# First stage of a gated cross-attention block worked by halves of its batches, with its loads reordered

## Chip, cores and metric

One core of a Trainium2 chip runs the whole program; the other cores are idle. The metric is device time in microseconds (us), the median over runs. The trace is of one profiled execution.

## What is computed

Two layers of cross-attention and a feed-forward part each. Only the first attention matters here (8 batches, 100 tokens, 361 context rows, width 256):

```
h = layernorm(x)                                   # x (8, 100, 256)
s = (h Wq^T + bq)(ctx Wk^T + bk)^T / 16            # ctx (8, 361, 256)
p = softmax(where(mask, s, -1e9))
x = x + tanh(g_xattn[0]) * (p (ctx Wv^T + bv))
x = x + tanh(g_ffn[0]) * ffn(layernorm(x))         # experts, next stage
...                                                # second layer
```

## The kernel before

Each engine has its own instruction list, written out by hand, and waits on semaphores where it needs another's result. The first stage avoids the keys: it forms `fold` = Wq^T Wk / 16 once (L1499, called from the `mm` helper: four products of 256 columns), and the small vectors `foldv` and `fold0` from the biases (ten products with one column each). With them the score of a batch is `tT` times the raw context, where `tT` = fold^T `hT` + `foldv`, plus a constant per token, `ccol`.

In order, the stage does this:

- **SyncE** issues all loads in one queue: `x` (100 partitions of 8 KB), `consts`, the three weights `wq0`, `wk0`, `wv0` (tile `arena` in the trace), `bqk`, the gates, the row `bv`, `mask8`, and then the context of batches 0-1, 2-3 and 4-7 (`GROUPS`, `load_context`): each as two pieces of its transpose (`ctxT`, in `ctxbuf`) and three of its rows (`ctxN`, in `big`, 121, 121 and 119 partitions). After that come rows and weights of the next stage.
- **VectorE** takes the statistics of all eight batches (L1068, L1056), GpSimd raises the variance to -1/2 (L606), and VectorE writes the normed rows `hN` (L1063).
- **TensorE** waits for all of `ld_w0` (64) and `ld_const` (64), forms the fold and the bias products, transposes `hN` in four groups of two batches (`ln_pe`, L1509), each of which ScalarE copies to `hT` (L763), and then makes four query groups of 400 columns (`tT`, copied by ScalarE, L776), two rows of constants (`cT`, one output row of 400 columns each, L780) and eight tiny transposes that turn the constants into `ccol` (L1547, L1081).
- Then a loop over i runs scores(i) against `ctxT`, softmax on VectorE and ScalarE (L1090 to L1094, L795), and for earlier batches the transpose of the probabilities, the mix with the context rows, its transpose and the product with `wv0`. Before scores(0), (2) and (4) TensorE waits for the context group (`ld_ctx0` to `ld_ctx2`).

A product of float32 shows as two MATMUL records in the trace, a transpose as one. `arena`, `ctxbuf` and `big` are shared by many tiles.

## Time and profile before

| | us |
|---|---|
| median of 3 runs | 556.81 (556.79 to 558.48) |
| the profiled execution's own time | 556.68 |
| its span in the trace | 554.9 |
| TensorE busy | 503.3 (91%) |
| VectorE busy | 277.3 (50%) |
| ScalarE busy | 188.4 (34%) |
| GpSimd busy | 160.9 (29%) |
| hardware DMA queue, share of 16 engines | 42.2% |

The span is what the trace covers; the 1.8 us beside it lie outside the records. The busy share says which engine sets most of the time; what the change is worth is read from the first 33 us.

### The profile page before, as it was taken

Reading aid. Unit: us, or ns where it says so; the run is one execution under the profiler, and the core shown is the slowest. Engines: PE = TensorE matmul, PEld = TensorE weight load, DVE = VectorE, ACT = ScalarE, POOL = GpSimd, SP = SyncE. Lnnn points to the kernel's source line nnn. Section 1 sums busy time; section 2 is a strip of 40 time slices with the busy share of each in tenths; the row PEclk is TensorE's granted clock in tenths of the full one; section 3 lists DMA queues with packets and bytes.
Section 4 is the critical chain, followed back from the end, with each engine's and each line's share of the span. In section 5 each row is a group of like instructions: output and inputs, shape, how many; then the busy total and the mean of one; then the engine's idle time right before and its main releaser. Section 6 shows DMA issues by size and latency. Waiting matters only on the chain.

```text
span 554.9 us, 9313 instructions
## 1 busy us (share of the span) xinstructions
PE 503.3 (91%) x3392; PEld 334.6 (60%) x3392; DVE 277.3 (50%) x664; ACT 188.4 (34%) x443; POOL 160.9 (29%) x179
## 2 busy tenths in 40 slices
PE   1989889899999889999999989899999988999992
PEld 1636565445556558887877767778867564444441
DVE  2436553112222767565576877988743214323452
ACT  1233331121112436555555554646652103110000
POOL 3122005001016306422241562543200666000232
PEclk9799978999999999999999999999999997999997
DMA  8978992269976987887555209300000233002100
GB/s 220 220 200 282 389 335 57 80 215 395 386 258 210 257 187 211 217 203 186 144 138 138 55 2 332 124 2 2 2 1 0 68 129 121 18 17 68 27 11 24
DMA packets 51790, 82.33 MB, mean 148 GB/s; under 512 B 10340, under 2 KB 40428, under 8 KB 51643
## 3 DMA queue, kind: packets, MB, share of 16 engines
q1 hardware_dynamic: 45967, 69.58, 42.2%
q0 software_dynamic: 5776, 12.13, 6.9%
q8 instruction: 29, 0.48, 0.4%
q14 instruction: 18, 0.15, 0.1%
HBM read 66.87 MB, written 15.15 MB: 148 GB/s over the span
## 4 chain that ended last, share of the span: by engine, by line
PE 73%; DVE 12%; issue 4%; DMA 4%; ACT 2%; SPq 1%; POOL 1%; POOLq 0%; DVEq 0%; ACTq 0%
PE pb L1499 68%; DVE hN L1063 2%; DVE nmx L1360 1%; DMA row_bv<-in_L_xattn_bv 1%; DMA qx_dram<-big_r 1%; DVE prob L1363 1%; PE pb L1910 1%; DMA hN<-yt_dram 1%; DVE bn L1050 1%; POOL rstd L606 1%; PE pb L1770 1%; DVE ctxbuf L1290 1%; PE pb L1680 1%; DVE nmx L1268 1%; DVE x L1211 1%
## 5 line engine op out<-in xcount | busy, mean ns | idle before, releaser
L1499 PE MATMUL pb<-split 128*100 128x362 f32 (+2 forms) x320 | 77.5, 326 | 4.0 <-DVE nmx L1268 2.7
L1499 PE MATMUL pb<-ring,big 128*116 (+1 forms) x232 | 76.8, 578 | 1.1 <-ACT big L822 1.1
L1268 DVE TENSOR_REDUCE nmx<-pb 100x1 f32<-100x361 f32 x128 | 62.8, 527 | 21.4 <-PE pb L1499 20.9
L1499 PEld LDWEIGHTS pb<-split 128*100 128x100 f32 (+2 forms) x320 | 55.5, 181 | 13.7 <-DVE nmx L1268 5.3
L1499 PEld LDWEIGHTS pb<-ring,big 128*116 128x116 f32 (+1 forms) x232 | 31.2, 162 | 43.2 <-issue 40.6
L939 ACT ACTIVATE big<-pb 121x400 f32<-121x400 f32 (+1 forms) x96 | 48.3, 505 | 20.5 <-PE pb L1499 17.9
L691 POOL TENSOR_TENSOR shift<-consts,nmx 100x400 fp32r<-100x400 f32 x32 | 28.2, 882 | 75.0 <-DVE nmx L1268 74.9
L1499 PE MATMUL pb<-big,arena 121*32 121x100 f32 (+3 forms) x1072 | 47.4, 261 | 1.7 <-ACT arena L789 1.2
L1499 PEld LDWEIGHTS pb<-big,arena 121*32 121x32 f32 (+3 forms) x1072 | 28.7, 112 | 18.2 <-issue 6.9
L1499 PE MATMUL pb<-hT,wgu 128*128 128x400 f32 (+1 forms) x100 | 35.8, 505 | 0.3 <-DVE hN L1346 0.3
L1499 PE MATMUL pb<-shift 100*121 100x400 f32 (+1 forms) x96 | 35.0, 364 | 0.0
L606 POOL TENSOR_TENSOR rstd<-std,minus_half 100x2 f32<-100x2 f32 (+3 forms) x11 | 11.0, 1000 | 71.9 <-DVE std L1058 46.0
L1499 PE MATMUL pb<-wdn,big 128*100 128x256 f32 x128 | 29.2, 380 | 1.4 <-issue 1.4
L1499 PE MATMUL pb<-ctxbuf 128*100 128x100 f32 x256 | 28.0, 253 | 0.0
L1499 PE MATMUL pb<-big,ring 128*128 128x464 f32 x64 | 27.8, 596 | 0.2 <-DVE big L1468 0.2
L1499 PEld LDWEIGHTS pb<-ctxbuf 128*100 128x100 f32 x256 | 26.1, 168 | 1.4 <-issue 0.8
L1499 PEld LDWEIGHTS pb<-hT,wgu 128*128 128x128 f32 x100 | 19.5, 206 | 12.1 <-issue 3.1
L660 POOL TENSOR_TENSOR ctxbuf<-tT,consts 128x1600 f32<-128x1600 f32 x8 | 24.4, 3045 | 7.4 <-PE pb L1499 7.4
L1499 PEld LDWEIGHTS pb<-wdn,big 128*100 128x100 f32 x128 | 20.8, 167 | 7.4 <-issue 2.0
L638 POOL DMA_INDIRECT yt_dram<-arena,tok x8 | 7.8, 978 | 59.3 <-ACT arena L841 59.3
L1499 PE MATMUL pb<-arena 128*100 128x256 f32 (+1 forms) x40 | 11.9, 433 | 13.6 <-DMA row_bv<-in_L_xattn_bv 12.0
L982 ACT ACTIVATE prob<-prob 100x400 f32<-100x400 f32 x32 | 17.2, 539 | 19.5 <-DVE prob L1363 19.2
(274 smaller groups left out, 844.1 us busy)
## 6 DMA issues: line engine op xcount, KB each, us to landing
ring<-in_L_ffn_gate_up_proj SPq DMA_DIRECT2D x12, 1024.0 KB, 10.1
split<-kx_dram SPq DMA_DIRECT2D x64, 181.0 KB, 3.9
ring<-in_L_ffn_down_proj SPq DMA_DIRECT2D x12, 512.0 KB, 7.9
kx_dram<-split POOLq DMA_DIRECT2D x16, 362.0 KB, 4.0
ctxbuf<-in_L_ffn_gate_up_proj SPq DMA_DIRECT2D x4, 1024.0 KB, 10.3
ring<-in_L_ffn_W_experts SPq DMA_DIRECT2D x4, 1024.0 KB, 13.3
split<-qx_dram SPq DMA_DIRECT2D x64, 50.0 KB, 2.1
ctxbuf<-in_ctxT SPq DMA_DIRECT2D x6, 361.0 KB
```

Source lines behind the costliest of these rows:

```text
L606: nc.gpsimd.tensor_tensor(to[:, a:z], var[:, a:z], minus_half[0:var.shape[0], a:z], ALU.pow) \
L638: nc.gpsimd.indirect_dma_start(yt_dram, bass.IndirectOffsetOnAxis(tok[:, i:i + 1], 0), yb[:, i % 2, :], None, bounds_check=NT - 1, oob_is_ ...
L660: nc.gpsimd.tensor_tensor(qbd[:, b % 2].rearrange("p k (h t) -> p k h t", h=8), q, m, ALU.mult) \
L691: nc.gpsimd.tensor_tensor(diag[:, t % 2].rearrange("t (h q) -> t h q", h=4), ident[0:T, 0:T].unsqueeze(1).to_broadcast([T, 4, T]), nmx[:, ...
L939: nc.scalar.activation(pTq[0:KEYS_OF[j], t % 2, j, :], PB[ST[j]][0:KEYS_OF[j], 0:4 * T], ACT.Exp) \
L982: nc.scalar.activation(prob4[:, n % 3, :], prob4[:, n % 3, :], ACT.Exp).then_inc(s("d_p"), 1)
L1050: nc.vector.bn_stats(bn6[:, b, :], x[:, b, :]).then_inc(s("stats"), 1)
L1063: nc.vector.tensor_scalar(hN[:, b, :], x[:, b, :], mv[:, b, 0:1], rstd[:, b:b + 1], ALU.subtract, ALU.mult).then_inc(s("n_hN"), 1)
L1211: nc.vector.scalar_tensor_tensor(out=x[:, b, :], in0=hN[:, b, :], scalar=tg[0:T, 2:3], in1=x[:, b, :], op0=ALU.mult, op1=ALU.add).then_inc ...
L1268: nc.vector.tensor_reduce(nmx[:, t % 4, q:q + 1], PB[SB[n % 3]][0:T, 0:CTX], AX.X, ALU.max, negate=True) \
L1290: link(nc.vector.tensor_tensor(w4, w4, sin, ALU.mult))
L1499: return nc.tensor.matmul(o, l, r, start=start, stop=stop)
```

## The change

The halves are batches 0-3 and 4-7.

- `by16` splits a load over partitions at the last multiple of 16: 100 becomes 96 and 4, 121 becomes 112 and 9, 119 becomes 112 and 7. It is applied to `x`, the mask and the context rows.
- SyncE loads `x` by halves and only the identity of `consts`; the gates, `wq0`, `wk0` and `bqk` are issued by ScalarE, which does so before anything else. SyncE then waits for the first half of `x`. `wv0` and the rest of `consts` are issued behind the context of batches 2-3 and counted with it; the context comes in four groups of two batches.
- Statistics, root and normed rows go by halves. ScalarE instead of VectorE copies the fold out, released by its own count, ahead of the bias products.
- TensorE first multiplies ones by ones, `WARM` = 20 times. Then it makes the queries of the first half between the transposes, and the two rows of constants between the queries.
- TensorE no longer waits for `ccol` before scores(0).

The diff, without what only renames or recounts semaphores:

```diff
+def by16(rows):
+    return [(0, rows // 16 * 16), (rows // 16 * 16, rows)]
...
-GROUPS = [(0, 2), (2, 4), (4, NB)]
+GROUPS = [(0, 2), (2, 4), (4, 6), (6, NB)]
+BESIDE = [0, 16 * 2, 0, 0]
...
+WARM = 20
...
-        LN_PARTS = dict(a=[(0, NB)], b=[(0, NB - 2), (NB - 2, NB)], c=[(0, NB // 2), (NB // 2, NB)], d=UNITS,
+        LN_PARTS = dict(a=[(0, NB // 2), (NB // 2, NB)], b=[(0, NB - 2), (NB - 2, NB)], c=[(0, NB // 2), (NB // 2, NB)], d=UNITS,
...
         @block.sync
         def _(sp):
-            sp.dma_start(x[:], A["x"]).then_inc(s("ld_x"), 16)
-            sp.dma_start(consts[:], A["consts"]).then_inc(s("ld_const"), 16)
-            for i, n in enumerate(("L0_xattn_Wq", "L0_xattn_Wk", "L0_xattn_WvT")):
-                sp.dma_start((wq0, wk0, wv0)[i][:], A[n].rearrange("(k p) n -> p k n", p=128)).then_inc(s("ld_w0"), 16)
-            sp.dma_start(bqk[:], A["bqk"]).then_inc(s("ld_w0"), 16)
+            for a, z in by16(T):
+                sp.dma_start(x[a:z, 0:NB // 2], A["x"][a:z, 0:NB // 2]).then_inc(s("ld_x"), 16)
+            for a, z in by16(T):
+                sp.dma_start(x[a:z, NB // 2:], A["x"][a:z, NB // 2:]).then_inc(s("ld_const"), 16)
+            sp.dma_start(ident, A["consts"][:, cs["ident"]]).then_inc(s("ld_const"), 16)
             def load_context(g):
                 a, z = GROUPS[g]
...
                     sp.dma_start(ctxT[:, k, a:z, 0:CTX], A["ctxT"][128 * k:128 * k + 128, a:z]).then_inc(s(f"ld_ctx{g}"), 16)
                 for j in range(NJ):
                     n = min(KEYS, CTX - KEYS * j)
-                    sp.dma_start(ctxN[0:n, a:z, j, :], A["ctx"][a:z, KEYS * j:KEYS * j + n, :].rearrange("b p d -> p b d")) \
-                        .then_inc(s(f"ld_ctx{g}"), 16)
-            for i, n in enumerate(("g_xattn", "g_ffn")):
-                sp.dma_start(gates[:, 2 * i:2 * i + 2], A[n].partition_broadcast(128)).then_inc(s("ld_const"), 16)
-            sp.dma_start(brow["bv"][:], A["L0_xattn_bv"].partition_broadcast(128)).then_inc(s("ld_const"), 16)
-            sp.dma_start(mask8[:], A["mask"]).then_inc(s("ld_mask"), 16)
+                    for p, q in by16(n):
+                        sp.dma_start(ctxN[p:q, a:z, j, :], A["ctx"][a:z, KEYS * j + p:KEYS * j + q, :].rearrange("b p d -> p b d")) \
+                            .then_inc(s(f"ld_ctx{g}"), 16)
             sp.wait_ge(s("filled"), FILL["pads"])
-            for g in range(len(GROUPS)):
+            sp.wait_ge(s("ld_x"), 32)
+            for a, z in by16(T):
+                sp.dma_start(mask8[a:z], A["mask"][a:z]).then_inc(s("ld_mask"), 16)
+            sp.dma_start(brow["bv"][:], A["L0_xattn_bv"].partition_broadcast(128)).then_inc(s("ld_mask"), 16)
+            load_context(0)
+            load_context(1)
+            sp.dma_start(wv0[:], A["L0_xattn_WvT"].rearrange("(k p) n -> p k n", p=128)).then_inc(s("ld_ctx1"), 16)
+            sp.dma_start(consts[:, 128:], A["consts"][:, 128:]).then_inc(s("ld_ctx1"), 16)
+            for g in range(2, len(GROUPS)):
                 load_context(g)
             for n, w in (("bo", "L1_xattn_bo"), ("n1", "L1_ffn_norm1_w"), ("n2", "L1_ffn_norm2_w")):
-                sp.dma_start(brow[n][:], A[w].partition_broadcast(128)).then_inc(s("ld_small"), 16)
+                sp.dma_start(brow[n][:], A[w].partition_broadcast(128)).then_inc(s("ld_wb"), 16)
             sp.dma_start(wr[:], A["L0_ffn_w_routerT"].rearrange("(k p) n -> p k n", p=128)).then_inc(s("ld_wb"), 16)
             for i, n in enumerate(("L0_ffn_w_gateT", "L0_ffn_w_upT")):
...
             pool.wait_ge(s("filled"), FILL["ones"])
...
                     nc.scalar.activation(hT[:, :, 2 * T * g:2 * T * (g + 1)], bank3(g % 2, KT, 2 * T), ACT.Copy) \
                         .then_inc(s("n_hT"), 1)
+            for i, n in enumerate(("g_xattn", "g_ffn")):
+                nc.scalar.dma_start(gates[:, 2 * i:2 * i + 2], A[n].partition_broadcast(128)).then_inc(s("ld_gates"), 16)
+            for w, n in ((wq0, "L0_xattn_Wq"), (wk0, "L0_xattn_Wk")):
+                nc.scalar.dma_start(w[:], A[n].rearrange("(k p) n -> p k n", p=128)).then_inc(s("ld_w0"), 16)
+            nc.scalar.dma_start(bqk[:], A["bqk"]).then_inc(s("ld_w0"), 16)
             act.wait_ge(s("filled"), FILL["ones"])
-            act.wait_ge(s("ld_const"), 64)
-            nc.scalar.activation(tg[:], gates[:], ACT.Tanh).then_inc(s("act_step"), 1)
-            ln_act("a")
-            for u in range(2 * KT):
-                n, half = u // 2, u % 2
+            act.wait_ge(s("ld_gates"), 32)
+            nc.scalar.activation(tg[:], gates[:], ACT.Tanh).then_inc(s("a_csb"), 1)
+            act.wait_ge(s("a_fold"), 1)
+            nc.scalar.activation(fold[:], bank3(2, KT, D), ACT.Copy, scale=1.0 / 16).then_inc(s("a_foldsb"), 1)
+            ln_act("a", range(0, 2))
+            def query_copy(u):
+                half, n = u // KT, u % KT
                 act.wait_ge(s("a_t"), u + 1)
-                if u == 0:
-                    act.wait_ge(s("a_foldsb"), 1)
                 nc.scalar.activation(tT[:, n, HALF * half:HALF * (half + 1)], PB[4 + u % 2][:, 0:HALF], ACT.Identity,
                                      bias=foldv[:, n:n + 1]).then_inc(s("a_tsb"), 1)
-            for half in range(2):
+            def constant_copy(half):
                 act.wait_ge(s("a_c"), half + 1)
                 nc.scalar.activation(cT[:, HALF * half:HALF * (half + 1)], PB[6 + half][0:1, 0:HALF], ACT.Identity,
                                      bias=fold0[:]).then_inc(s("a_csb"), 1)
+            act.wait_ge(s("a_ccsb"), 1)
+            query_copy(0)
+            ln_act("a", range(2, 3))
+            query_copy(1)
+            ln_act("a", range(3, 4))
+            constant_copy(0)
+            query_copy(2)
+            constant_copy(1)
+            query_copy(3)
             act.wait_ge(s("filled"), FILL["pads"])
             for i in range(NB + 4):
                 if 2 <= i < NB + 2:
...
-            dve.wait_ge(s("ld_x"), 16)
-            for b in range(NB):
+            dve.wait_ge(s("ld_x"), 32)
+            for b in range(NB // 2):
                 nc.vector.bn_stats(bn6[:, b, :], x[:, b, :]).then_inc(s("stats"), 1)
             ln_variance("a", 0)
             ln_rows("a", 0)
-            dve.wait_ge(s("a_fold"), 1)
-            nc.vector.tensor_scalar(fold[:], bank3(2, KT, D), 1.0 / 16, None, ALU.mult)
+            dve.wait_ge(s("ld_const"), 48)
+            for b in range(NB // 2, NB):
+                nc.vector.bn_stats(bn6[:, b, :], x[:, b, :]).then_inc(s("stats"), 1)
+            ln_variance("a", 1)
+            dve.wait_ge(s("a_fold"), 2)
             nc.vector.tensor_scalar(foldv[:], PB[3][:, 0:4], 1.0 / 16, None, ALU.mult)
-            nc.vector.tensor_scalar(fold0[:], PB[3][0:1, 4:5], 1.0 / 16, None, ALU.mult).then_inc(s("a_foldsb"), 1)
-            dve.wait_ge(s("act_step"), 1)
-            dve.wait_ge(s("ld_const"), 64)
+            nc.vector.tensor_scalar(fold0[:], PB[3][0:1, 4:5], 1.0 / 16, None, ALU.mult).then_inc(s("a_ccsb"), 1)
+            ln_rows("a", 1)
+            dve.wait_ge(s("a_csb"), 1)
+            dve.wait_ge(s("ld_mask"), 48)
             link(nc.vector.tensor_scalar(grow[:], brow["bv"][0:T], tg[0:T, 0:1], None, ALU.mult))
             link(nc.vector.tensor_tensor(x[:], x[:], grow[:].unsqueeze(1).to_broadcast([T, NB, D]), ALU.add))
             dve.wait_ge(s("a_cc"), 1)
             nc.vector.tensor_copy(ccol[:], PB[3][0:T, 0:NB]).then_inc(s("a_ccsb"), 1)
-            dve.wait_ge(s("a_ccsb"), 1)
+            dve.wait_ge(s("a_ccsb"), 2)
...
-            pe.wait_ge(s("ld_w0"), 64)
-            pe.wait_ge(s("ld_const"), 64)
+            pe.wait_ge(s("filled"), FILL["ones"])
+            for _ in range(WARM):
+                mm(PB[7][:, 0:128], ones[:, 0:128], ones[:, 0:128], True, True)
+            pe.wait_ge(s("ld_w0"), 48)
             for m in range(KT):
                 for k in range(KT):
-                    mm(PB[2][:, m * D:(m + 1) * D], wq0[:, k, 128 * m:128 * m + 128], wk0[:, k, :], k == 0, k == KT - 1)
+                    last = mm(PB[2][:, m * D:(m + 1) * D], wq0[:, k, 128 * m:128 * m + 128], wk0[:, k, :], k == 0, k == KT - 1)
+            last.then_inc(s("a_fold"), 1)
...
             last.then_inc(s("a_fold"), 1)
-            ln_pe("a")
-            pe.wait_ge(s("a_foldsb"), 1)
-            pe.wait_ge(s("n_hT"), NB // 2 * (turn("a") + 1))
-            for u in range(2 * KT):
-                n, half = u // 2, u % 2
+            pe.wait_ge(s("ld_const"), 48)
+            ln_pe("a", range(0, 2))
+            def queries(u):
+                half, n = u // KT, u % KT
+                pe.wait_ge(s("n_hT"), NB // 2 * turn("a") + 2 * (half + 1))
                 if u >= 2:
                     pe.wait_ge(s("a_tsb"), u - 1)
                 for m in range(KT):
                     last = mm(PB[4 + u % 2][:, 0:HALF], fold[:, m, 128 * n:128 * n + 128],
                               hT[:, m, HALF * half:HALF * (half + 1)], m == 0, m == KT - 1)
                 last.then_inc(s("a_t"), 1)
-            for half in range(2):
+            def constants(half):
+                pe.wait_ge(s("a_ccsb"), 1)
                 for m in range(KT):
                     last = mm(PB[6 + half][0:1, 0:HALF], foldv[:, 2 + m:3 + m], hT[:, m, HALF * half:HALF * (half + 1)],
                               m == 0, m == KT - 1)
                 last.then_inc(s("a_c"), 1)
-            pe.wait_ge(s("a_tsb"), 2 * KT)
-            pe.wait_ge(s("a_csb"), 2)
-            pe.wait_ge(s("filled"), FILL["ones"])
+            pe.wait_ge(s("a_foldsb"), 1)
+            queries(0)
+            ln_pe("a", range(2, 3))
+            queries(1)
+            ln_pe("a", range(3, 4))
+            constants(0)
+            queries(2)
+            constants(1)
+            queries(3)
+            pe.wait_ge(s("a_csb"), 3)
             for b in range(NB):
                 last = nc.tensor.transpose(PB[3][0:T, b:b + 1], cT[0:1, T * b:T * b + T], ident[0:1, 0:1])
             last.then_inc(s("a_cc"), 1)
-            pe.wait_ge(s("a_ccsb"), 1)
+            pe.wait_ge(s("a_tsb"), KT)
             for i in range(NB + 4):
                 if 2 <= i < NB + 2:
                     b = i - 2
                     pe.wait_ge(s("a_p"), b + 1)
+                    if b == 0:
+                        pe.wait_ge(s("a_tsb"), 2 * KT)
+                    if b == 1:
+                        pe.wait_ge(s("a_ccsb"), 2)
                     if b >= 2:
                         pe.wait_ge(s("a_ptsb"), b - 1)
                     for j in range(NJ):
...
                         pe.wait_ge(s("a_max"), b - 2)
                     for g, (a, z) in enumerate(GROUPS):
                         if a == b:
-                            pe.wait_ge(s(f"ld_ctx{g}"), 16 * (KT + NJ))
+                            pe.wait_ge(s(f"ld_ctx{g}"), 16 * (KT + 2 * NJ) + BESIDE[g])
                     for n in range(KT):
                         last = mm(PB[SB[b % 3]][0:T, 0:CTX], tT[:, n, T * b:T * b + T], ctxT[:, n, b, 0:CTX],
                                   n == 0, n == KT - 1)
```

How the order moves. **TensorE**, from the transposes of group 2 of `hN` to the first scores, of the kernel before (`consts,hN` are transposes, `hT,arena` are queries, `hT,foldv` constants, `consts,sil` the tiny transposes, `ctxbuf,tT` scores):

```order
L1509 MATMUL pb<-consts,hN 128x100 [waits n_hT,n_hN]
L1509 MATMUL pb<-consts,hN 128x100 x3
L1509 MATMUL pb<-consts,hN 128x100 [waits n_hT,n_hN]
L1509 MATMUL pb<-consts,hN 128x100 x3
L1499 MATMUL pb<-hT,arena 128x400 [waits n_hT,a_foldsb]
L1499 MATMUL pb<-hT,arena 128x400 x3
L1499 MATMUL pb<-hT,arena 128x400 [waits a_tsb]
L1499 MATMUL pb<-hT,arena 128x400
L1499 MATMUL pb<-hT,arena 128x400 [waits a_tsb]
L1499 MATMUL pb<-hT,arena 128x400
L1499 MATMUL pb<-hT,foldv 1x400 x4
L1547 MATMUL pb<-consts,sil 100x1 [waits filled,a_csb,a_tsb]
```

And now, from the first query on (the transposes of groups 0 and 1 stand right ahead of it; lines are the changed kernel's):

```order
L1535 MATMUL pb<-hT,arena 128x400 [waits n_hT,a_foldsb]
L1535 MATMUL pb<-hT,arena 128x400
L1545 MATMUL pb<-consts,hN 128x100 [waits n_hT,n_hN]
L1545 MATMUL pb<-consts,hN 128x100 x3
L1535 MATMUL pb<-hT,arena 128x400 [waits n_hT]
L1535 MATMUL pb<-hT,arena 128x400
L1545 MATMUL pb<-consts,hN 128x100 [waits n_hT,n_hN]
L1545 MATMUL pb<-consts,hN 128x100 x3
L1535 MATMUL pb<-hT,foldv 1x400 [waits a_ccsb]
L1535 MATMUL pb<-hT,foldv 1x400
L1535 MATMUL pb<-hT,arena 128x400 [waits a_tsb,n_hT]
L1535 MATMUL pb<-hT,arena 128x400
```

The transposes of group 2 and of group 3 now stand behind the first and second query, and the constants between the queries. **SyncE**, its loads of the kernel before up to the first pieces of context:

```order
L403 DMA x<-in_x 100x2048
L404 DMA consts<-in_consts 128x493
L406 DMA arena<-in_L_xattn_Wq 128x2x256
L406 DMA arena<-in_L_xattn_Wk 128x2x256
L406 DMA arena<-in_L_xattn_WvT 128x2x256
L407 DMA bqk<-in_bqk 128x4
L419 DMA gates<-in_g_xattn 128x2
L419 DMA gates<-in_g_ffn 128x2
L420 DMA row_bv<-in_L_xattn_bv 128x256
L421 DMA mask<-in_mask 100x2888
L412 DMA ctxbuf<-in_ctxT 128x2x361 x2
```

And now:

```order
L413 DMA x<-in_x 96x1024
L413 DMA x<-in_x 4x1024
L415 DMA x<-in_x 96x1024
L415 DMA x<-in_x 4x1024
L416 DMA consts<-in_consts 128x128
L432 DMA mask<-in_mask 96x2888
L432 DMA mask<-in_mask 4x2888
L433 DMA row_bv<-in_L_xattn_bv 128x256
L421 DMA ctxbuf<-in_ctxT 128x2x361 x2
L425 DMA big<-in_ctx 112x2x256
L425 DMA big<-in_ctx 9x2x256
L425 DMA big<-in_ctx 112x2x256
```

The weights and gates are gone from this queue, `x` and the context rows come in more pieces, and mask and `bv` stand behind a wait (for the first half of `x`).

## Rows read from the trace of the kernel before

**Rows 1.** Waits of TensorE, whole span: engine line <- releaser: us in total, times, longest.

```profile
PE pb L1499 <- DMA row_bv<-in_L_xattn_bv: 12.0, 1, 12.0
```

**Rows 2.** Chain of waits in order of time: start us, us, what.

```profile
20.83 10.77 PE pb L1499 x24
31.60 0.72 issue
...
33.17 1.47 PE pb L1499 x4
```

**Rows 3.** Timeline of TensorE: start us, us, engine line op out<-in xcount.

```profile
12.03 3.63 PE L1499 MATMUL pb<-arena 128*128 128x256 f32 x8 [12.03 <-DMA row_bv<-in_L_xattn_bv]
...
15.49 1.84 PE L1499 MATMUL pb<-bqk,arena 128*128 128x1 f32 x16
...
17.43 0.91 PE L1509 MATMUL pb<-consts,hN 100*128 100x100 f32 x8
...
20.83 7.99 PE L1499 MATMUL pb<-hT,arena 128*128 128x400 f32 x16 [0.69 <-ACT hT L763]
...
32.33 0.52 PE L1547 MATMUL pb<-consts,sil 1*100 1x1 f32 x8 [0.72 <-issue]
```

**Rows 4.** Windows: PE, PEld, DVE, ACT, POOL busy, PEclk, DMA share, GB/s.

```profile
0.00:2.00 2.00, 0.00 (x0) 0.00 (x0) 0.00 (x0) 0.00 (x0) 1.45 (x7) 1.00 0.24 37
2.00:4.00 2.00, 0.00 (x0) 0.00 (x0) 0.00 (x0) 0.00 (x0) 1.35 (x6) 1.00 0.57 175
4.00:6.00 2.00, 0.00 (x0) 0.00 (x0) 0.00 (x0) 0.00 (x0) 0.00 (x0) 1.00 1.07 251
6.00:8.00 2.00, 0.00 (x0) 0.00 (x0) 0.00 (x0) 0.00 (x0) 0.00 (x0) 1.00 0.98 224
...
18.81:25.64 6.83, 6.14 (x16) 3.56 (x16) 2.13 (x1) 1.73 (x4) 0.00 (x0) 0.50 1.03 231
25.64:31.60 5.96, 5.96 (x18) 2.11 (x16) 0.00 (x0) 2.38 (x4) 0.00 (x0) 1.00 0.76 222
```

**Rows 5.** Timeline of GpSimd, VectorE and ScalarE, same columns.

```profile
0.73 0.40 POOL L592 MEMSET ones<- 128x363 f32 x1 [0.29 <-POOLq L2023]
...
8.16 2.71 DVE L1068 BATCH_NORM_STATS2 bn<-x 100x6 f32<-100x256 f32 x8 [8.16 <-DMA x<-in_x]
...
11.91 1.68 POOL L606 TENSOR_TENSOR rstd<-std,minus_half 100x8 f32<-100x8 f32 x1 [8.56 <-DVE std L1058]
...
13.63 3.67 DVE L1063 TENSOR_SCALAR hN<-x,mv,rstd 100x256 f32<-100x256 f32 x8 [1.87 <-POOL rstd L606]
...
18.03 0.90 ACT L763 ACTIVATE hT<-pb 128x400 f32<-128x400 f32 x2 [4.57 <-PE pb L1509]
```

**Rows 6.** Timeline of TensorE, full rate: a 256-column group of eight.

```profile
116.86 1.89 PE L1499 MATMUL pb<-wdn,big 128*100 128x256 f32 x8
```

**Rows 7.** Timeline of TensorE: scores of batches 2 and 6.

```profile
37.69 1.38 PE L1499 MATMUL pb<-ctxbuf,tT 128*100 128x361 f32 x4
...
52.15 1.38 PE L1499 MATMUL pb<-ctxbuf,tT 128*100 128x361 f32 x4
```

**Rows 8.** Windows as in Rows 4, longer stretches.

```profile
0.00:12.00 12.00, 0.00 (x0) 0.01 (x1) 3.52 (x17) 0.04 (x1) 2.88 (x13) 1.00 0.81 215
12.00:20.00 8.00, 7.63 (x44) 6.64 (x44) 6.10 (x13) 2.84 (x5) 3.58 (x5) 0.93 0.87 222
20.00:29.00 9.00, 8.31 (x18) 4.14 (x18) 0.94 (x1) 2.45 (x6) 0.00 (x0) 0.69 0.97 229
29.00:32.00 3.00, 2.60 (x8) 0.50 (x6) 0.00 (x0) 1.41 (x3) 0.00 (x0) 1.00 0.72 245
32.00:45.00 13.00, 10.79 (x51) 6.57 (x51) 6.71 (x13) 4.16 (x14) 4.12 (x8) 1.00 0.84 223
```

**Rows 9.** Timeline, SyncE's issues of context rows of batches 2 and 3, three pieces.

```profile
13.42 3.87 SPq L415 DMA_DIRECT2D big<-in_ctx  x3
```

**Rows 10.** Windows as in Rows 4, the later stretch at half clock.

```profile
76.84:87.08 10.24, 10.24 (x33) 7.12 (x33) 5.91 (x24) 2.94 (x4) 1.19 (x1) 0.50 0.53 188
```

More of the change, by code:

```diff
@@ L610, in _ @@
             inverse_root("a")
-            pool.wait_ge(s("ld_mask"), 16)
+            pool.wait_ge(s("ld_mask"), 48)
             for b in range(NB):
@@ L1617, in _ @@
             ln_pe_b(range(3))
-            pe.wait_ge(s("ld_wb"), 64)
+            pe.wait_ge(s("ld_wb"), 112)
             logits(range(6))
@@ L1697, in _ @@
             pe.wait_ge(s("ld_wc"), 16 * 7)
-            pe.wait_ge(s("ld_ctx0"), 16 * (KT + NJ + KT))
+            pe.wait_ge(s("ld_ctx0"), 16 * (KT + 2 * NJ + KT))
             def keys_values(piece, bank):
```

10 lines of the change are left out of this document (5 added, 5 removed).

## Prediction

> **What bounds the kernel now.** I read four views. First TensorE's waits over the span: the only long one is at the start, 12.0 us for the row `bv` [rows 1], although no product needs `bv`; it is counted in `ld_const` with things that are needed. Second the chain of waits: from 12.03 us it stays almost wholly on TensorE, through 24 records of queries and constants (20.83 to 31.60), a gap of 0.72 and the tiny transposes to the first scores at 33.17 [rows 2]. Third TensorE's timeline of that piece [rows 3], for the price of each step. Fourth windows for the clock and the transfers [rows 4, 8]. The reader is to see that before 33.17 us other engines are never the last for long, that the first 12 us are empty, and that the queries ran at two speeds: PEclk is 0.50 (1.2 GHz) from 18.81 to 25.64 and 1.00 (2.4 GHz) after [rows 4]. PEclk is not to be trusted for the very first products: it says 1.00, but eight records of 256 columns took 3.63 us, 0.454 each [rows 3], and records of the same width later take 1.89/8 = 0.236 [rows 6]. They ran at the lower level.
>
> All later work follows the scores in the same order, so what the change is worth is how much earlier the first scores start, if their context is there.
>
> **The change, part by part.**
>
> Arrival of the weights. Needed are now `x` (800 KB), the identity (64), `wq0` and `wk0` (512) and 4 KB of small ones: 1380 KB, or 1.41 MB. The kernel before moved 0.07, 0.35, 0.50 and 0.45 MB in its first four windows of 2 us, 1.37 MB by 8.0 [rows 4]. At that pace the 1.41 MB are in at 8.2 us. Bounds: 12.0 if the second queue brings nothing, since all was in by then [rows 1]; and about 6 if the weights, being 0.5 MB of it, overtake half of `x` (0.92 MB landed at 6.2 by the same windows). I take 8.2, the nearest row being the bytes themselves. The Trainium skill ("DMA: Bandwidth & Descriptors", Issuing engines are not separate DMA queues) says that issuing from several engines saves sequencer time only, since all share the same DMA engines. It speaks against ScalarE's queue as such and agrees with pricing by bytes; the gain here is what no longer stands ahead.
>
> Warm-up products. Twenty are 40 records with 128x128 weights and 128 columns, from 1.1 us, when the ones are filled [rows 5]. The trace has none; the nearest are the bias products, same weights, one column: 16 in 1.84, 0.115 each at full clock [rows 3], so 4.6 us and an end at 5.7; at half clock twice that, an end at 10.3. The products before ran at half clock for at least 12.03 to 15.49 [rows 3], so I take 3.5 us at 0.23 (15 records) and 25 at 0.115: an end at 7.5, covered by the wait for weights. If the clock rises later they end up to 2 us after the weights and cost that. I start the fold at 8.3: -3.7 us.
>
> The fold. Eight records took 12.03 to 15.49 = 3.46; at full clock 8 x 0.236 = 1.9 [rows 3, 6]: -1.55. Bound above: no gain if the clock is low. Now 10.2.
>
> Bias products: 15.49 to 17.43 = 1.94 [rows 3], bound by weight loads, unchanged: 12.15. The copy of the fold (moved to ScalarE) lies beside them and beside the transposes; cover gone, it would cost about 0.7.
>
> First transposes. Before, four groups and their copies took 17.43 to 20.83 = 3.4 [rows 2, 3]. Now two groups precede the first query: 2 x 0.46 (0.91 for eight, [rows 3]), one copy of 0.45 [rows 5] and hops, 1.55: -1.85, at 13.7. Are the rows there? First half of `x` by about 5 us (its 0.4 MB with an equal share of weights, [rows 4]); from the first statistics to the first normed row it took 13.63 - 8.16 = 5.5 for eight batches, so at least half of that and rather 3.5 for four, then rows 4 x 0.46 [rows 5]: ready at about 10.4. VectorE then queues the second statistics and the copy of `foldv`, which waits for the bias products (12.15), and rows 4-7 by 14.4; group 2 is due at 15.0. Both fit; late next would be `foldv`.
>
> Queries and constants. Before 10.77 for 24 records [rows 2]. At full clock a record of 400 columns is 5.96/18 = 0.331 [rows 4]: 7.95, and two groups of transposes now stand between, 0.9. Sum 8.85: -1.9, at 22.55. ScalarE's copies lie beside them.
>
> Tail. Before 31.60 to 33.17 = 1.57: last constant copied, tiny transposes, copy by VectorE. Now the constants are followed by a query that covers their copy, and scores(0) doesn't wait for `ccol`: 0.6, from the 0.52 of the transposes [rows 3]: -0.95.
>
> Sum: -3.7 - 1.55 - 1.85 - 1.9 - 0.95 = -9.95; the first scores start at 23.2.
>
> Context. Scores(2) came 4.5 us and scores(6) 19.0 us after the first [rows 2, 7], so groups 1 and 3 are due at 27.7 and 42.2. Ahead of them stand 5.24 and 8.20 MB. The windows moved 2.58 MB by 12, 4.36 by 20, 6.42 by 29, 7.15 by 32 and 223 GB/s after [rows 8]: 5.24 is in at 23.8, 8.20 at 36.7. Mask and `bv` lie in the first 3.3 MB, in at 15. Margins of 4 and 5.5 us: cost nothing. The same skill page (Why a DMA increments its semaphore by 16) says that a transfer uses the largest number of engines up to 16 that divides its slowest dimension: 10 for 100 partitions, 11 and 7 for 121 and 119. By it the pieces of 96 and 112 use all 16 and the margins grow; no row of the views shows engines apart.
>
> After the stage: weights of the next are behind the same bytes and TensorE never waited for them, so nothing is given back. What can move is the clock: it was 0.50 from 76.84 to 87.08 [rows 10]; another place or length of such stretches is worth up to some 4 us less (half of 10.24, short of what small work there would not gain), or 1.7 more (half of a stretch a third as long).
>
> 556.68 - 9.95 = 546.7; the median stands 0.13 above the profiled execution, so **546.9**. A measurement here tells about 0.3% (1.7 us) from no change.
>
> **Rivals.**
>
> *B, the clock is lost again before the queries.* Before, it fell at 18.81, after the one-column products and the transposes with their gap [rows 3, 4]; the same products still stand there. 3.4 us at half clock cost 1.7, 6.8 cost 3.4: 548.6 to 550.3. Against it: the fold at full clock stands right ahead, and gaps are shorter. The Trainium skill ("TensorE: Matmul & The Clock Gate", What's actually happening) says the throttled state is the default and activity lifts it; by it 20 products in front are no lasting gain.
>
> *C, context or weights late.* Two queues share the engines and the 19 small pieces add packets of their own. If the pace is 180 GB/s instead of about 223, 8.20 MB are in at 45.6, 3.4 late: about 550; weights at 11 give much the same. For it: even before, 12 to 29 us ran at only 222 to 229 while asked for more [rows 8].
>
> *D, issue-bound, slower.* SyncE has 37 issues from the mask to the last context piece, starting at 5 when the half of `x` is in. Context issues of two batches took 3.87/3 = 1.29 each [rows 9]. If that is a price per issue and not back-pressure of bytes, the last goes out at 5 + 37 x 1.29 = 52.7 and lands 2 or more later, 54.7 against 52.15 when scores(6) ran before [rows 7]: 559.4. It decides above (52.15 - 7)/37 = 1.22 per issue. Against it: a small piece has 18 rows, not 242.
>
> *E, no gain.* The time is won and given back to a transfer of the next stages: 556.5. No row shows such a wait.
>
> **How the numbers follow.** A 0.58 (own range 544.5 to 548.6: earlier weights, clock elsewhere), B 0.22, C 0.13, E 0.03, D 0.04. The range must reach through B and most of C, and below A by what the later clock stretches may give: 543.5 to 551.5, leaving out D, E and tails, some 0.15. Faster by over 0.3%: A, B, C, 0.93; same 0.03; slower 0.04.
>
> **What would show it.** Right: first fold record at 8 to 9 us at 0.24 each; PEclk 1.00 from the fold to the scores; first scores at 22.5 to 24; no TensorE wait on context; the stretch after them of equal length. B: PEclk 0.50 within the queries and records of 0.667. C: a wait on `in_ctx` or `in_ctxT`. D: SyncE's issues above 1.2 us each. I am wrong if the scores start at 23 and the total is not about 10 lower.

## Result, and the profile after

| | before | changed |
|---|---|---|
| median | 557.44 (6 runs) | 552.6 (6 runs, 551.01 to 559.98) |
| profiled execution, and its span | 556.68, 554.9 | 554.01, 552.2 |
| first scores start | 33.17 | 31.48 |

The ratio is 0.9906, with a 95% interval of 0.9887 to 0.9925: faster, but by 4.8 us and not by the 10 forecast, and just outside the range. (The run of 559.98 had a mean granted clock of 0.954 against 0.966 to 0.972 in the other five, and is left out of the ratio.) In a second set of six runs (a2, below) it was 0.9899 (0.9859 to 0.994).

The timeline of TensorE in the changed kernel, to be laid beside [rows 3]:

```profile
1.24 6.94 PE L1535 MATMUL pb<-ones 128*128 128x128 f32 x40 [1.24 <-POOL minus_half L608]
11.66 2.78 PE L1535 MATMUL pb<-arena 128*128 128x256 f32 x8 [3.48 <-DMA bqk<-in_bqk]
14.24 3.41 PE L1535 MATMUL pb<-bqk,arena 128*128 128x1 f32 x16
17.57 0.24 PE L1535 MATMUL pb<-bqk 128*1 128x1 f32 x4
17.74 1.59 PE L1545 MATMUL pb<-consts,hN 100*128 100x100 f32 x8
20.02 3.01 PE L1535 MATMUL pb<-hT,arena 128*128 128x400 f32 x4 [0.69 <-ACT hT L778]
...
23.23 1.53 PE L1535 MATMUL pb<-hT,arena 128*128 128x400 f32 x4
...
30.99 0.55 PE L1597 MATMUL pb<-consts,sil 1*100 1x1 f32 x8
31.48 2.67 PE L1535 MATMUL pb<-ctxbuf,tT 128*100 128x361 f32 x8
```

Two things stand there. The ones end at 8.18 us, and then TensorE waits 3.48 us for the last load of ScalarE's queue. And the sixteen bias products take 3.41 us instead of 1.84 [rows 3], the first query 3.01 instead of the 1.53 of the next: half clock. The windows say the same (columns as in [rows 4]):

```profile
2.00:4.00 2.00, 2.00 (x12) 2.00 (x11) 0.00 (x0) 0.00 (x0) 1.35 (x6) 1.00 0.63 181
4.00:6.00 2.00, 2.00 (x12) 2.00 (x11) 1.12 (x4) 0.00 (x0) 0.00 (x0) 1.00 0.30 69
6.00:8.00 2.00, 2.00 (x20) 1.98 (x18) 0.84 (x6) 1.09 (x1) 0.94 (x1) 1.00 1.02 280
...
12.72:17.74 5.02, 5.02 (x25) 4.60 (x23) 0.12 (x1) 0.60 (x1) 3.02 (x5) 0.50 1.12 254
17.74:22.96 5.22, 4.54 (x16) 2.83 (x14) 4.06 (x8) 1.01 (x2) 0.00 (x0) 0.50 1.11 268
22.96:31.50 8.54, 8.54 (x38) 3.68 (x36) 0.00 (x0) 4.14 (x8) 0.00 (x0) 1.00 1.10 280
```

PEclk is 0.50 (1.2 GHz) from 12.72 to 22.96. And from 4 to 6 us the core moved 69 GB/s, where the kernel before moved 251 [rows 4]: the transfers nearly stopped while the weights were wanted. What was issued when, and how long it took to land:

```profile
0.73 0.42 ACTq L782 DMA_DIRECT2D gates<-in_g_xattn  x1
...
2.67 0.49 ACTq L785 DMA_DIRECT2D bqk<-in_bqk  x1
```

```profile
arena<-in_L_xattn_Wk ACTq DMA_DIRECT2D x1, 256.0 KB, 8.0
...
gates<-in_g_xattn ACTq DMA_DIRECT2D x1, 1.0 KB, 4.3
gates<-in_g_ffn ACTq DMA_DIRECT2D x1, 1.0 KB, 5.7
bqk<-in_bqk ACTq DMA_DIRECT2D x1, 2.0 KB, 8.9
```

The first fence is ScalarE's timeline, the second the DMA issues of the first 12 us (KB, then us to landing). Two loads of 1 KB, broadcast to 128 partitions in 8-byte pieces, needed 4.3 and 5.7 us at the head of the queue, and 2 KB at its end 8.9. What each queue moved from 2 to 6 us (packets, MB, share of 16 engines; q1 is SyncE's queue, q10 ScalarE's):

```profile
q1 hardware_dynamic: 141, 0.50, 42.5%
q10 hardware_dynamic: 283, 0.00, 3.8%
```

ScalarE's queue moved 283 packets and almost no bytes in these 4 us: the weights behind the gates had hardly begun.

### The profile page after: what moved, and what is told of

It reads as the page before. It is cut to its first block, busy times and chain, and to the rows that moved or that the text cites. A ratio compares the mean times of both kernels' runs of the same rounds, so it can differ in the third digit from the quotient of the medians.

```text
span 552.2 us, 9422 instructions
## 1 busy us (share of the span) xinstructions
PE 508.8 (92%) x3432; PEld 340.5 (62%) x3432; DVE 276.5 (50%) x664; ACT 188.4 (34%) x444; POOL 161.4 (29%) x180
## 4 chain that ended last, share of the span: by engine, by line
PE 63%; issue 20%; DMA 6%; DVE 5%; SPq 2%; ACT 2%; POOL 1%; ACTq 0%; POOLq 0%; DVEq 0%
PE pb L1535 59%; DMA ctxbuf<-es_dram 2%; SPq L573 2%; DMA bqk<-in_bqk 2%; DMA hN<-yt_dram 1%; DVE hN L1095 1%; PE pb L1824 1%; PE pb L1545 1%; PE pb L1734 1%; DVE x L1247 1%; DVE bn L1082 1%; POOL ctxbuf L675 1%; PE pb L1709 0%; POOL rstd L621 0%; ACT hT L778 0%
## 5 line engine op out<-in xcount | busy, mean ns | idle before, releaser
L1535 PEld LDWEIGHTS pb<-split 128*100 128x100 f32 (+2 forms) x320 | 54.2, 177 | 13.4 <-DVE nmx L1304 5.5
L1535 PE MATMUL pb<-hT,wgu 128*128 128x400 f32 (+1 forms) x100 | 33.9, 483 | 0.3 <-DVE hN L1382 0.3
L621 POOL TENSOR_TENSOR rstd<-std,minus_half 100x4 f32<-100x4 f32 (+2 forms) x12 | 11.4, 949 | 72.9 <-DVE std L1090 47.0
L1535 PE MATMUL pb<-wdn,big 128*100 128x256 f32 x128 | 29.2, 380 | 1.4 <-DVE big L1413 1.4
L1535 PEld LDWEIGHTS pb<-hT,wgu 128*128 128x128 f32 x100 | 18.5, 195 | 11.1 <-issue 1.3
L1535 PE MATMUL pb<-wc,ctxbuf 128*121 128x256 f32 x96 | 23.6, 383 | 0.0
```

The lines of the kernel that those rows point to most:

```text
L621: nc.gpsimd.tensor_tensor(to[:, a:z], var[:, a:z], minus_half[0:var.shape[0], a:z], ALU.pow) \
L1535: return nc.tensor.matmul(o, l, r, start=start, stop=stop)
```

## The experiments

All ratios are to runs of the kernel before on the same chip. The kernel before had medians of 557.44 to 560.77 us in these sets, so a kernel with the same time can get another ratio (the changed kernel has 552.6 us and 0.9906, e2 below 552.71 us and 0.986): differences of some 0.5% between variants of different sets are not resolved. "Fold at" is the start of TensorE's first fold product. Two questions stood open at first. Why are the weights late: because of the gates ahead of them, because of mask and context beside them, or because a second queue is slow in itself? And why does the clock fall: because of the gap before the fold, or because of the one-column bias products?

**Order of ScalarE's queue: gates last (e1).** The two gate loads go behind `bqk`:

```diff
-            for i, n in enumerate(("g_xattn", "g_ffn")):
-                nc.scalar.dma_start(gates[:, 2 * i:2 * i + 2], ...
             for w, n in ((wq0, "L0_xattn_Wq"), (wk0, "L0_xattn_Wk")):
...
             nc.scalar.dma_start(bqk[:], A["bqk"]).then_inc(s("ld_w0"), 16)
+            for i, n in enumerate(("g_xattn", "g_ffn")):
+                nc.scalar.dma_start(gates[:, 2 * i:2 * i + 2], ...
```

> Changed kernel with the two gate loads issued by ScalarE behind the weights and bqk instead of ahead of them. Theory 'small packets' (256 packets of 8 bytes at the head of ScalarE's queue leave the engines nearly idle from 4 to 6 us, 69 GB/s there): the weights are in at 9 to 9.5 us instead of 11.6, the window 4 to 6 us moves over 200 GB/s, total 2 to 5 us below the changed kernel. Theory 'late loads' (mask, bv and context, issued from 4.9 us, take the engines from the weights): the start of the fold stays at 11 to 11.7, total within 1 us.

Measured 549.83 us (547.9 to 553.3), ratio 0.9811 (0.9738 to 0.9883). A window of it, its queue q10 from 2 to 6 us, and its timeline:

```profile
4.00:6.00 2.00, 2.00 (x11) 2.00 (x11) 0.14 (x1) 0.00 (x0) 0.00 (x0) 1.00 1.13 316
```

```profile
q10 hardware_dynamic: 555, 0.52, 46.7%
```

```profile
9.34 1.99 PE L1535 MATMUL pb<-arena 128*128 128x256 f32 x8 [0.61 <-DMA bqk<-in_bqk]
...
14.75 3.00 PE L1535 MATMUL pb<-hT,arena 128*128 128x400 f32 x4 [0.74 <-ACT hT L778]
```

316 GB/s where 69 were, and 0.52 MB on ScalarE's queue where there was next to nothing: the tiny loads ahead of the weights were what held the weights up, and the fold starts 2.3 us earlier. Yet the first query is at half clock again (3.00): a gap of 0.61 instead of 3.48 did not save the clock in this execution.

**What shares the engines: SyncE waits for the weights (e3).** One line; mask, value bias and context are issued only when the weights are in.

```diff
-            sp.wait_ge(s("ld_x"), 32)
+            sp.wait_ge(s("ld_w0"), 48)
```

> Changed kernel where SyncE waits for the weights (ld_w0) instead of the first half of x before mask, bv and context. 'Late loads': weights in at 9 to 9.5 us, total 1 to 4 us lower unless context is then late. 'Small packets': weights at 11 or later as before, everything behind them 5 us later, context late at scores(2) or (6), total the same or higher.

Measured 551.7 us (549.77 to 552.44), ratio 0.9834 (0.9778 to 0.9891). Fold at 10.04; the core then moves little until the context gets going, and still no product waits for it:

```profile
4.00:6.00 2.00, 2.00 (x11) 2.00 (x11) 1.55 (x6) 0.00 (x0) 0.00 (x0) 1.00 0.41 134
...
10.00:12.00 2.00, 1.96 (x10) 1.75 (x11) 1.47 (x8) 0.00 (x0) 0.38 (x1) 1.00 0.46 103
```

This lies between what the two theories said (9 to 9.5, or 11 and later). Four executions of the changed kernel (below) started the fold at 11.04 to 11.66, 11.33 on average; against that mean the sharing cost 1.3 us of the arrival and the order of the queue 2.0, each by one execution. This execution, with a gap of 1.24 us before the fold and the plain bias products, kept full clock to the scores (25.46).

**The products of ones: 32 and none (e2, e4).** `WARM = 20` becomes 32, or 0.

> Changed kernel with 32 products of ones instead of 20. Theory 'clock lost in the gap' (TensorE idle from 8.2 to 11.65 brings the half clock back at 12.7): the ones end at about 11.5 to 12, the clock stays 1.00 through fold, biases and queries, first scores at 26 to 27.5 instead of 31.5, total about 4 us below the changed kernel. Rival 'lost by the one-column products' (the biases and transposes themselves bring it down): PEclk 0.50 again within the queries, total 0 to 1.5 us lower.

> Changed kernel without the products of ones. If they bring only the first records of the fold at full clock: fold 3.46 instead of 2.78, the clock rises within the biases as it did in the kernel before, total within 1.5 us of the changed kernel, either way. If they carry the clock through the stage: total 3 us or more above it.

With 32 the ones end 0.64 us before the fold, and this execution keeps full clock to the scores at 26.63, which gives every step at its full rate:

```profile
11.21 1.99 PE L1535 MATMUL pb<-arena 128*128 128x256 f32 x8 [0.64 <-DMA bqk<-in_bqk]
13.04 1.84 PE L1535 MATMUL pb<-bqk,arena 128*128 128x1 f32 x16
...
14.99 0.90 PE L1545 MATMUL pb<-consts,hN 100*128 100x100 f32 x8
16.63 1.58 PE L1535 MATMUL pb<-hT,arena 128*128 128x400 f32 x4 [0.74 <-ACT hT L778]
...
26.63 2.67 PE L1535 MATMUL pb<-ctxbuf,tT 128*100 128x361 f32 x8
```

Its median is 552.71 (550.56 to 555.08), ratio 0.986 (0.9795 to 0.9925), not to be told from the changed kernel's; the 4 us that the theory of the gap expected did not come. With none, 555.07 (551.96 to 558.26), ratio 0.9888 (0.9816 to 0.9959): fold at 11.46 in 3.75 us, bias products in 3.41, scores at 32.49. With weights that come at 11 to 11.7 us no gain by the ones can be told from these runs: the ranges of the two kernels overlap.

**One queue (e7).** All loads are SyncE's: rows of the first half, both weights, `bqk`, rows of the second, identity, gates; ScalarE issues none.

```diff
+            for w, n in ((wq0, "L0_xattn_Wq"), (wk0, "L0_xattn_Wk")):
+                sp.dma_start(w[:], ...).then_inc(s("ld_w0"), 16)
+            sp.dma_start(bqk[:], A["bqk"]).then_inc(s("ld_w0"), 16)
             for a, z in by16(T):
                 sp.dma_start(x[a:z, NB // 2:], ...
             sp.dma_start(ident, ...
+            for i, n in enumerate(("g_xattn", "g_ffn")):
+                sp.dma_start(gates[:, 2 * i:2 * i + 2], ...
```

> Changed kernel with all loads on SyncE's queue: first half of x, the two weights, bqk, second half of x, identity, gates. Theory 'small packets at the head of a second queue': with the bytes in order the weights (0.94 MB with half of x) are in at 7 us or soon after, TensorE starts the fold when the ones end, 8.3 to 8.8; first scores at 24 if the clock holds, 27 if not; total 3 to 5 us below the changed kernel. Theory 'two queues are needed' (descriptors come at a fixed rate per queue): weights at 9 or later.

Measured 546.92 us (545.36 to 549.26), ratio 0.9784 (0.9742 to 0.9827): some 5 to 6 us under the changed one, and with e14 (below) the fastest kernel here; two later executions of it (e12, e13) took 550.77 and 548.11 us. A window and its timeline:

```profile
4.00:6.00 2.00, 2.00 (x18) 2.00 (x18) 1.31 (x4) 0.00 (x0) 0.00 (x0) 1.00 1.01 313
```

```profile
1.23 6.24 PE L1535 MATMUL pb<-ones 128*128 128x128 f32 x40 [1.23 <-POOL minus_half L613]
7.31 1.89 PE L1535 MATMUL pb<-arena 128*128 128x256 f32 x8
...
12.90 1.58 PE L1535 MATMUL pb<-hT,arena 128*128 128x400 f32 x4 [1.01 <-ACT hT L783]
...
22.91 2.67 PE L1535 MATMUL pb<-ctxbuf,tT 128*100 128x361 f32 x8
```

The fold follows the ones with no wait, so in this execution the weights are in by 7.31 (in e10, below, which has no ones and waits for them, at 7.88). The gates now stand behind all that is due early. A second queue with the gates last (e1, 9.34; e5, below, 8.78 or sooner) was not quicker than the one queue; no run has the order of e7 on two queues, so what the second queue itself costs or gives is not shown.

**Is the loss by the clock the kernel's or one execution's? (a2, a3, a4, e12, e13)** The changed kernel profiled three times more, the one queue twice more, unchanged.

> The changed kernel as it stands, beside the three that follow, so that they are compared on one chip. Both theories: fold starts at 11.7 us, the clock falls at about 12.7 us, first scores at 31.5 us, end at 552 us; time 552 to 554 us, 3 to 7 us below the kernel before.

> The changed kernel, a further profiled execution. Theory that the gap of 2.4 to 3.5 us between the products of ones and the fold costs the clock: PEclk 0.50 somewhere between 12 and 24 us again, for 3.4 to 10.3 us, first scores at 28 to 31.5 us. Rival, that it is a matter of the execution alone: no fall before the scores in one of the two, first scores at 26.5.

> One queue for all loads, a second profiled execution. Theory that products of ones which run into the fold keep the clock: no fall before 23 us, first scores at 22.9 us. Rival, that the one-column bias products cost it in some executions whatever stands ahead: first scores at 24.6 us or later, with PEclk 0.50 from 13 to 17 us, in one of the two.

(The texts for the fourth execution, and for the third of one queue, say the same.) The second execution missed its text: the clock fell at 17.03 us, not at 12.7, and the scores came at 28.13, not 31.5. From the timelines and windows of each:

| | fold | half clock before the scores | first scores | end of span |
|---|---|---|---|---|
| changed, 1st | 11.66 | 12.72 to 22.96 | 31.48 | 552.2 |
| changed, 2nd | 11.04 | 17.03 to 20.45 | 28.13 | 553.1 |
| changed, 3rd | 11.14 | 17.36 to 20.77 | 28.25 | 547.3 |
| changed, 4th | 11.48 | 12.47 to 22.71 | 31.30 | 552.4 |
| one queue, 1st | 7.31 | none | 22.91 | 543.6 |
| one queue, 2nd | 7.93 | 12.54 to 19.37 | 26.27 | 549.0 |
| one queue, 3rd | 8.25 | 13.23 to 16.65 | 25.09 | 546.3 |

The theory of the gap says that one queue never falls; it fell in two of three, with no gap ahead of the fold. The windows of its second execution:

```profile
5.71:12.54 6.83, 6.79 (x57) 6.35 (x56) 4.52 (x23) 2.32 (x4) 2.13 (x3) 1.00 0.94 250
12.54:19.37 6.83, 6.13 (x12) 3.37 (x13) 4.82 (x6) 1.66 (x4) 1.93 (x4) 0.50 1.12 255
```

TensorE was busy for 6.79 of the 6.83 us before it fell; the last 2.9 of them were one-column products and transposes. A busy TensorE did not keep the clock there. Nor is the gap cleared: in the changed kernel, where it was 3.4 us, half clock lasted 10.2 us and the bias products themselves were slow; where it was 2.4, 3.4 us. All twelve executions here that have ones and the plain bias products can be laid side by side. With a gap of over 2 us (the four, and e6 below) five of five lost the clock before the scores; with a gap of 1.3 us or less e1, e8, e12 and e13 lost it, and e2, e3 and e7 kept it. So a long gap goes with the loss, and a short one leaves it open which way an execution goes.

What stands behind the scores matters as much. The second and third execution of the changed kernel start the scores at 28.13 and 28.25 and end 5.8 us apart; their mean granted clocks are 0.966 and 0.977, which is 12 us more at half clock in the one, so some 6 us.

**Wide products between the bias products (e5, e9, e14, e15).** Behind each of the four pairs of bias products one product of ones:

```diff
                            k == 0, k == KT - 1)
+                    mm(PB[7][:, 0:256], ones[:, 0:128], ones[:, 0:256], True, True)
```

e5 is this with e1, e14 and e15 (the same kernel twice) with one queue; e9 is one queue with 128 columns.

> Gates behind the weights, as in e1, and one more product of ones with 256 columns behind each of the four pairs of bias products. Theory 'the one-column products lose the clock': with wide products between them PEclk stays 1.00 from the fold to the scores; the biases take 1.9 us longer (eight records of 0.236), first scores at 9.3 + 15.4 + 1.9 = 26.6 against 27.7 in e1, total about 1 us below e1 on average. Rival 'it is the gap before the fold': the clock falls once again at about 14, first scores at 29 or later.

> One queue for all loads, and behind each of the four pairs of bias products one product of 128 columns of ones. If the one-column bias products can still cost the clock when the weights are early, this kernel differs from e7 in the executions that lose it, and its times lie closer together; if they cannot, it is e7 plus the four products. Fold at 7.3 us, biases 1 us longer than in e7 at most (four products of 128 columns and their waits), first scores 22.9 to 24, total within 1 us of e7's 546.9.

> One queue, and behind each of the four pairs of bias products one product of ones with 256 columns, twice as wide as in e9. If the one-column products cost the clock: no fall before the scores in either of the two executions, biases 0.6 us longer than in e9 at most, first scores at 24 to 25 us, every execution within 2 us of the others and a total at or below e7's. Rival, that what happened in e7 and e9 is a matter of when in an execution the clock is decided on, whatever stands there: a fall at 12.5 to 14 us in one of the two, first scores at 26 to 28 us there, times spread over 5 us as in e9.

| | columns | half clock before the scores | first scores | us | ratio |
|---|---|---|---|---|---|
| e5 | 256 | none | 26.03 | 549.33 | 0.9822 (0.9775 to 0.9869) |
| e9 | 128 | 13.76 to 20.59 | 27.73 | 549.13 | 0.9816 (0.9771 to 0.9862) |
| e14 | 256 | none | 25.60 | 547.03 | 0.9761 (0.9728 to 0.9794) |
| e15 | 256 | none | 25.21 | 547.79 | 0.9791 (0.9752 to 0.9829) |

All three executions with 256 columns kept the clock, the profiled one with 128 lost it, and its text (fold at 7.3, a total within 1 us of e7's) was missed. But three of seven executions with the plain products and a short gap kept it too, so three of three may still be luck, and that the one-column products cost the clock is not shown. The stretch from fold to first query is 7.14 us instead of 5.59, and first scores miss the 24 to 25 expected:

```profile
8.45:15.59 7.14, 6.41 (x46) 5.51 (x45) 4.28 (x18) 2.87 (x5) 3.09 (x5) 1.00 0.97 254
```

The wide products cost what they save: from fold to first scores e14 and e15 take 17.15 us each, the three executions of one queue without them 16.9 on average, and the totals agree. The times do lie closer together: eleven of the twelve runs lie within 546.27 to 548.89 (the twelfth is 551.71), against 545.36 to 550.77 in the eight of one queue without wide products and 545.09 to 551.98 in e9's six.

e9's runs show what the clock can decide: 551.59, 551.27 and 551.98 at a mean granted clock of 0.966, and 546.83, 546.99 and 545.09 at 0.975, 0.974 and 0.978. At 0.966 some 2 x 0.034 x 550 = 37 us are at half clock, at 0.975 27: 10 us more of them, 5 us of time. It does not decide everything: the kernel before took 557.12 and 562.03 us on the same chip, both at 0.969.

**One queue without ones (e10), and only the loads (e11).** e10 is e7 with `WARM = 0`. e11 is the kernel before with its loads in the order rows, `wq0`, `wk0`, `bqk`, identity, gates, mask, `bv`, context, and `wv0` and the rest of `consts` behind the second context group.

> One queue for all loads and no products of ones. Theory that the warm-up is worth what it says once the weights are early: fold starts at about 7 us at half clock (3.75 us for 8 records instead of 1.9), biases at half clock 3.4 us, the clock rises a few us later, first scores at 26 to 28 us against 22.9, total 2 to 4 us above e7's 546.9. Rival, that the products of ones are worth nothing because the fold itself brings the clock up in time: first scores at 24 us at most, total within 1 us of e7.

> The kernel before with nothing changed but the order of its loads on the one queue: rows, both weights, bias, identity, gates, mask, value bias, context. No products of ones, whole-batch statistics, constants after all four groups of transposes. Theory that most of what one queue gives is the order of the loads: fold starts at 8 to 9 us instead of 12.03, first scores at about 29 to 30 us instead of 33.17, total 3 to 5 us below before. Rival, that the gain needs the new order of the queries and the warm products: total within 1.5 us of before.

e10: 551.67 us (548.32 to 554.11), ratio 0.9875 (0.9838 to 0.9912). Fold at 7.88 in 3.36 us, scores at 26.08. With early weights the ones are worth some 0.009 of the time, 5 us, by medians on different chips, and 3.5 us by the means if e12 and e13 are counted in; 2 to 4 were expected. The profiled execution was the fastest of its six; its scores are 3.2 us later than in e7, but 1.3 later than the mean of the three executions of one queue (24.76).

e11: 556.98 us (554.31 to 557.76, 12 runs), ratio 0.9958 (0.9936 to 0.9981), 1.4 us by the medians and 2.4 by the ratio, short of the 3 to 5 expected. Its timeline:

```profile
10.17 3.78 PE L1502 MATMUL pb<-arena 128*128 128x256 f32 x8 [10.17 <-DMA bqk<-in_bqk]
13.74 3.41 PE L1502 MATMUL pb<-bqk,arena 128*128 128x1 f32 x16
...
21.12 8.32 PE L1502 MATMUL pb<-hT,arena 128*128 128x400 f32 x16 [0.69 <-ACT hT L766]
29.38 2.85 PE L1502 MATMUL pb<-hT,foldv 128*1 128x400 f32 x8
```

The fold starts 1.9 us earlier, the bias products take 3.41 against 1.84 [rows 3], and in this execution the scores are not earlier at all (33.80 against 33.17): half clock lasted from the fold through most of the queries, 8.32 us for 16 records, where in the one execution of the kernel before the bias products, from 15.49 us on, ran at full clock [rows 3]. So here the early loads were given back to the clock. It was profiled once, and in the median they still gained a little; that it needs the ones to keep them is likely by e7 against e10, but not shown for this kernel.

**Rows whole (e6).** The function `by16` returns one piece of all rows, with the semaphore counts to match.

> Changed kernel without the split at a multiple of 16: x, mask and context rows in whole pieces of 100, 121, 121 and 119 partitions. If the split is hidden, as in the prediction: no wait of TensorE on context, first scores within 1 us of the changed kernel's (31.5 at a half clock in the queries, 27 without), total within 1.5 us. If context is now near its limit: a wait before scores(2), (4) or (6), total 2 us or more above; the pace from 12 to 30 us falls from 255 to 280 GB/s to about 225.

Measured 551.03 us (549.68 to 551.57), ratio 0.9844 (0.9792 to 0.9896), which overlaps the changed kernel's. The windows of e6, the first from the time of the weights and two over the context loads, and then the changed kernel's of the latter:

```profile
4.00:6.00 2.00, 2.00 (x12) 2.00 (x12) 0.51 (x2) 0.00 (x0) 0.00 (x0) 1.00 0.83 214
...
20.00:30.00 10.00, 10.00 (x39) 4.11 (x37) 1.16 (x3) 3.35 (x6) 0.00 (x0) 1.00 0.94 237
30.00:45.00 15.00, 13.31 (x61) 8.71 (x61) 9.41 (x20) 6.06 (x19) 5.24 (x10) 1.00 0.82 232
```

```profile
20.00:30.00 10.00, 9.98 (x30) 4.45 (x31) 1.94 (x1) 3.60 (x7) 0.00 (x0) 0.85 1.11 275
30.00:45.00 15.00, 13.31 (x60) 7.76 (x59) 7.87 (x16) 5.19 (x16) 4.26 (x8) 1.00 1.03 289
```

The split raises the pace by a sixth to a quarter, and nothing waits for it. At the start it does harm. With rows whole, and the gates still ahead of the weights, the fold starts at 10.32, where seven executions with the rows split and the same order of loads (the four, e2, e4, e8) have 11.02 to 11.66. From 4 to 6 us e6 moves 214 GB/s where the changed kernel moves 69, and the two queues from 2 to 6 us are:

```profile
q1 hardware_dynamic: 228, 0.70, 57.4%
q10 hardware_dynamic: 234, 0.04, 8.2%
```

So ScalarE's queue was held up by the gates with either kind of rows (0.00 and 0.04 MB), while SyncE's moved 0.70 MB in this one execution and 0.50 in the changed kernel's, where `x` comes in pieces of 96 and 4. Why the two together nearly stop both queues isn't shown.

**Old order of queries and constants (e8).** All four groups of transposes first and the constants last, as before, with 32 products of ones.

> As e2 (32 products of ones), but with all four groups of transposes ahead of the four queries and both constants behind them, as in the kernel before. From fold to first scores e2 took 15.4 us at full clock. By my steps the order is worth: two groups and copies ahead of the first query (1.35 us of waiting) and the copy of the last constant in the tail (0.8): 17.5 here, first scores 2 us later than e2, total 2 us above e2. If the order is worth nothing: 15.4 to 16.

Measured 551.51 us (548.73 to 554.14), ratio 0.9845 (0.9784 to 0.9905); fold at 11.02, scores at 29.34, but at half clock from 15.5 to 22.3, so order and clock can't be parted by a difference of totals. Its records taken at their full rates (8 transposes and 4.9 us of queries at half clock) give about 3.2 us less, some 15.1 from fold to scores against e2's 15.42: an estimate, by which the new order of queries and constants is worth nothing. A run of it at full clock throughout wasn't obtained.

## Why the prediction was wrong, step by step

- **What bounds the kernel**: right. From the first scores to the end of the span the kernel before took 521.7 us, the four executions of the changed one 520.7, 525.0, 519.0 and 521.1; what moves the scores moves the end, give or take what the later clock stretches do, which is up to 6 us between two executions and so more than the whole gain.
- **Arrival of the weights** ("I start the fold at 8.3"): the step that failed first. It priced bytes by the pace of the kernel before, and asked of the gates only how many bytes they are. They held ScalarE's queue for the first 6 us, a price in time and not in bytes (e1: 2.0 us of the arrival); the mask and context were issued from 4.93 us on beside the weights (e3: 1.3 us); and the rows of `x` in pieces of 96 and 4, which the prediction took as a help, cost about 1 us (e6). Each was measured by one execution with the other two in place, so they are not to be added up. Four executions started the fold at 11.04 to 11.66, 3.0 us late on average. With one queue and the weights in order the fold starts as forecast: at 7.31, 7.93 and 8.25, right behind the ones. The bound "12.0 if the second queue brings nothing" was the nearer one.
- The Trainium skill ("DMA: Bandwidth & Descriptors", Issuing engines are not separate DMA queues) says that all loads run on the same DMA engines, whichever engine issues them. e7 agrees as far as it goes: all loads on one queue, in another order, were in sooner and not later.
- **Warm-up**: right. An end at 7.5 was forecast, and 8.18 came (8.05 to 8.76 in the other three), covered by the wait for the weights as forecast; the ones started every 0.21 us until 5.88, then every 0.11.
- **Fold, bias products, first transposes**: right at full clock. e2: 1.83 to the next step, 1.95 and 1.64, against 1.9, 1.94 and 1.55. What the new order of transposes, queries and constants itself gives is not shown: by the estimate from e8 next to nothing, where 2 us were expected.
- **Queries and constants** (8.85): mis-sized by 0.7. In e2 they take 26.15 - 16.63 = 9.52. The price of 0.331 a record came from 18 records counted in a window whose edges cut some of them; by e2's whole groups, start to start, it is about 0.36.
- **Tail** (0.6): 0.48 in e2. **Context**: right, and by a wider margin than forecast, since the pace rose to 275 to 289 GB/s. The Trainium skill ("DMA: Bandwidth & Descriptors", Why a DMA increments its semaphore by 16 and not by 1) says that the largest divisor up to 16 of the slowest dimension sets how many engines a load uses. The trace agrees: 237 GB/s from 20 to 30 us with rows whole, 275 with 112 and 9. (Rival C speaks of 19 small pieces; by the change there are 15: 2 of `x`, 1 of the mask, 12 of the context. Nothing was worked out from it.)
- **The clock**: the step that failed second ("PEclk 1.00 from the fold to the scores"). This was rival B, given 0.22. The clock fell before the scores in four executions of four, and cost about 18.5 - 15.4 = 3.0 us on average: 1.7 where half clock lasted 3.4 us, which is B's own price, and 4.4 where it lasted 10.2. What makes it fall stays open. The argument against it, "the fold at full clock stands right ahead, and gaps are shorter", is refuted by e12 and e13, which lost the clock behind a fold at full clock and without a gap before it. And B and C ("weights at 11") came together: each alone lay within the range, and both were not added up.
- **D and E**: neither came. SyncE's last context piece was issued by 29.2 us, not 52.7; no load of a later stage was waited for.

Sum for the first scores: forecast 23.2; arrival +3.0, clock +3.0, the sizes +0.5 give, unrounded, 29.8, the mean of the four. The median gained 4.8 where the scores of these executions are 3.4 earlier than in the one execution of before; the other 1.4 us are less than the spread that the later stretches make, and aren't explained further. That the total came out so near the range is partly luck of that spread.

## What to carry to other kernels

Price an early load by what stands ahead of it in its queue in time, not in bytes: a broadcast in 8-byte pieces belongs behind everything that is waited for, and here one queue in order of need served the weights better than two. Ask of a warm-up whether it runs into the real work: here it gave nothing measurable with late weights and 3.5 to 5 us with early ones. Where the clock can fall, one profile shows one outcome of several: profile the kernel more than once before a cause is read from it, and add rivals together where nothing excludes both.
